# Queries of batches 2 to 7 from a transposed x, with row statistics gathered once, in an attention and mixture-of-experts kernel

## The reference

```python
x = x + _L0_xattn_ref(_layernorm(x), ctx_1024, ctx_1024, Wq, Wk, Wv, Wo)
x = x + _L0_ffn_ref(_layernorm(x), gate_w, Wg, Wu, Wd, Ws_g, Ws_u, Ws_d)

# _L0_xattn_ref, with B, L, E = 8, 512, 256, H, D = 16, 16 and 1601 context rows
q = (query @ Wq.T).reshape(B, L, H, D) * scale
k = (key @ Wk.T).reshape(B, -1, H, D)
v = (value @ Wv.T).reshape(B, -1, H, D)
scores = sigmoid(einsum('blhd,bshd->bhls', q, k))
o = einsum('bhls,bshd->blhd', scores, v).reshape(B, L, E)
return o @ Wo.T
```

## Time and profile before

| | us |
|---|---|
| median of 3 runs | 1428.64 (1427.55 to 1428.79) |
| the profiled execution's own time | 1423.46 |
| its span | 1421.7 |
| PE busy | 1360.4, 96% |
| ACT busy | 957.4, 67% |
| DVE busy | 647.7, 46% |
| first stage, attention | from 0 to about 975 |

### The profile page before, as it was taken

The page is one execution under the profiler, slowest core; times in us unless marked ns, Lnnn a source line. Parts: engine busy times, 40 slices in busy tenths (PEclk is TensorE's granted clock), DMA queues, the critical chain, the costliest instruction groups (busy, mean ns, idle before and its releaser), DMA issues.

```text
span 1421.7 us, 22246 instructions
## 1 busy us (share of the span) xinstructions
PE 1360.4 (96%) x8906; PEld 783.3 (55%) x8906; DVE 647.7 (46%) x1294; ACT 957.4 (67%) x1073; POOL 211.2 (15%) x173
## 2 busy tenths in 40 slices
PE   4879999999999999999999999998999999999995
PEld 3434444444444435344444443325888888888885
DVE  4434244234235324424523531204449677777772
ACT  3547988888888887888888889994232344444441
POOL 1000000000000000000000000020000336666654
PEclk9989999999999999999999999999999999999998
DMA  6473765586387478467548627623343465666653
GB/s 171 122 164 112 118 126 148 107 150 156 101 136 161 127 124 147 137 118 149 146 109 135 170 69 122 134 73 133 132 132 108 134 175 148 150 151 148 149 97 38
DMA packets 97160, 185.82 MB, mean 131 GB/s; under 512 B 16992, under 2 KB 51296, under 8 KB 97056
## 3 DMA queue, kind: packets, MB, share of 16 engines
q1 hardware_dynamic: 80768, 154.08, 45.5%
q0 software_dynamic: 16000, 29.91, 10.2%
q10 hardware_dynamic: 288, 0.39, 0.2%
HBM read 118.99 MB, written 61.83 MB: 127 GB/s over the span
## 4 chain that ended last, share of the span: by engine, by line
PE 86%; ACT 4%; DVE 4%; issue 2%; DMA 2%; SPq 1%; POOL 0%; POOLq 0%; DVEq 0%
PE acc L1291 24%; PE score L1331 18%; PE score L1267 17%; PE score L1346 9%; PE misc L1182 6%; PE misc L1195 5%; ACT probs L679 4%; PE misc L1218 2%; PE misc L1203 2%; PE misc L1210 1%; DMA key_scr<-key_parts 1%; PE misc L1226 1%; DVE o_sum L859 1%; SPq L388 1%; PE acc L1358 1%
## 5 line engine op out<-in xcount | busy, mean ns | idle before, releaser
L679 ACT ACTIVATE probs<-score 128x1024 f32<-128x1024 f32 (+1 forms) x832 | 789.4, 1043 | 162.8 <-PE score L1267 158.0
L1291 PE MATMUL acc<-probs,values 128*32 128x512 f32 (+1 forms) x3328 | 411.2, 600 | 4.5 <-DVE o_sum L859 3.3
L1267 PE MATMUL score<-queries,keys 48*128 48x512 f32 (+1 forms) x1664 | 315.2, 451 | 3.4 <-DMA keys<-key_parts 2.4
L1267 PEld LDWEIGHTS score<-queries,keys 48*128 48x128 f32 (+1 forms) x1664 | 128.3, 180 | 258.1 <-ACT probs L679 201.5
L688 ACT ACTIVATE gelu<-score 128x512 f32<-128x512 f32 x96 | 57.1, 594 | 209.9 <-PE score L1331 209.8
L1291 PEld LDWEIGHTS acc<-probs,values 128*32 128x32 f32 (+1 forms) x3328 | 82.9, 109 | 183.8 <-issue 143.6
L576 POOL DMA_DIRECT2D ctx_raw<-ctx_t x32 | 23.4, 731 | 754.7 <-DVE ctx_lo L767 753.8
L778 DVE CAST key_parts<-misc 128x512 fp32r<-128x512 f32 (+1 forms) x63 | 36.2, 574 | 206.9 <-PE misc L1182 195.4
L1331 PE MATMUL score<-tok_hi,gu_hi 128*128 128x512 f32 x384 | 119.8, 393 | 0.0
L1331 PE MATMUL score<-tok_lo,gu_hi 128*128 128x512 f32 x384 | 119.3, 392 | 0.0
L1331 PE MATMUL score<-tok_hi,gu_lo 128*128 128x512 f32 x384 | 118.7, 391 | 0.0
(11 more groups left out here) (158 smaller groups left out, 1382.5 us busy)
## 6 DMA issues: line engine op xcount, KB each, us to landing
keys<-key_scr SPq DMA_DIRECT2D x180, 200.2 KB, 8.0
key_scr<-key_parts SPq DMA_DIRECT2D x45, 512.0 KB, 4.4
gu_raw<-w_gu SPq DMA_DIRECT2D x17, 1024.0 KB, 6.4
ctx_raw<-ctx_t POOLq DMA_DIRECT2D x24, 512.0 KB, 4.1
queries<-query_scr SPq DMA_DIRECT2D x180, 64.0 KB, 2.7
d_raw<-w_d SPq DMA_DIRECT2D x17, 512.0 KB, 9.0
query_scr<-query_parts SPq DMA_DIRECT2D x15, 512.0 KB, 4.5
xn<-x SPq DMA_DIRECT2D x8, 512.0 KB, 3.8
```

The source lines that it names most:

```text
L679: act.activation(probs[0:rows, n % RING, 2 * pair:2 * pair + 2, :], score[k % 3][0:rows, :, :], ACT.Sigmoid, scale=SCALE).then_inc(probs_d ...
L1267: mm = pe.matmul(score[k % 3][0:rows, g, :], keys[quarter % KEY_RING][of, pair, P * st:P * st + rows], queries[half][of, e, pair, :], star ...
L1291: mm = pe.matmul(acc[32 * c:32 * (c + 1), :], values[b % 2][0:rows, st, half, c, :], probs[0:rows, n % RING, c, :], start=(st == 0), stop= ...
```

## The change

The wrapper passes x a second time, transposed per batch (`x_t`). T tasks remain for batches 0 and 1 only. In batch 1 DVE reads the rows of the six batches 2 to 7 one after another through the one buffer `xn` and keeps their means and variances (`row_sums`, at q = 0, 3, 6, 9, 12, 15); SP issues the next load of x at q = 1, 4, 7, 10, 13, each once the sums before it are done. `row_scales` at q = 15 makes all the scales; a new task M at q = 17 transposes means and scales on PE, and SP writes them to DRAM. From then on SP, at task G of batch b, loads `x_t` of the next batch and two rows of 512 numbers broadcast to all partitions, and DVE at q = 29 norms the transposed x in place and splits it for Q, which moves from q = 30 to q = 35. The tasks behind it move too.

```diff
 def beside(b):
-        at_quad = (0, 2, 8, 10, 12, 14, 16, 18, *range(26, QPB, 2))
+        at_quad = (0, 2, 8, 10, 12, 14, 16, 18, 26, 28, 30, 32, 35, 37, 39, 42, 44)
...
-                 ("T", c, 0), ("T", c, 1), ("Q", c, 0),
+                 *([("T", c, 0), ("T", c, 1), ("Q", c, 0)] if c == 1 else []),
                  ("K", c, 0, 2), ("K", c, 1, 2), ("V", c, 2, 0), ("V", c, 2, 1),
+                 *([("Q", c, 0)] if c > 1 else []),
                  ("K", c, 0, 3), ("K", c, 1, 3), ("V", c, 3, 0), ("Q", c, 1)]
+    if b == 1:
+        tasks[STATS_AT + 2] = ("M",)
...
             def load_x(b):
-                sp.wait_ge(misc_copied, COUNT["T", b - 1, KC - 1])
+                if b <= 2:
+                    sp.wait_ge(misc_copied, COUNT["T", b - 1, KC - 1])
+                else:
+                    sp.wait_ge(x_summed, b - 2)
                 sp.dma_start(xn[:], x_rows[b]).then_inc(x_in, 16)
+            def load_x_t(b):
+                if b == 2:
+                    sp.wait_ge(x_summed, B - 2)
+                else:
+                    sp.wait_ge(x_t_split, b - 2)
+                sp.dma_start(x_turned, x_t[b].rearrange("(k p) s -> p k s", p=P)).then_inc(x_t_in, 16)
+            def load_stats(b):
+                sp.wait_ge(stat_written, 16)
+                sp.wait_ge(misc_copied, COUNT["G", b - 2])
+                sp.wait_ge(nt_stored, STORE * (b - 1))
+                for which in range(2):
+                    sp.dma_start(nt_lo[:, which, :].bitcast(F32),
+                                 stat_scr[which, b].rearrange("t p -> (t p)").partition_broadcast(P)
+                                 ).then_inc(stat_in, 16)
...
@@ SP, the loop over b and q @@
                         stack_keys(4 * b + 3)
+                    if b == 1 and 0 < q <= STATS_AT and q % STATS_STEP == 1:
+                        load_x(3 + q // STATS_STEP)
...
                         elif task == ("G", b - 1):
                             load_resid_a(b)
+                            if b + 1 < B:
+                                load_x_t(b + 1)
+                                load_stats(b + 1)
                             place_gates(b - 1)
...
+            def row_sums(b):
+                dve.wait_ge(x_in, 16 * (b + 1))
+                for t in range(TT):
+                    dve.bn_stats(x_bn[:, t, :], xn[:, t, :]).then_inc(ln_step, ln.up())
+                dve.wait_ge(ln_step, ln.now())
+                for t in range(TT):
+                    last = dve.bn_aggr(stat_mv[:, TT * b + t, :], x_bn[:, t, :])
+                last.then_inc(x_summed, 1)
+            def row_scales():
...
+                dve.tensor_copy(stat[:, 0, some], stat_mv[:, some, 0]).then_inc(stat_ready, 1)
+            def normed_queries(b):
+                dve.wait_ge(x_t_in, 16 * (b - 1))
+                dve.wait_ge(stat_in, 32 * (b - 1))
+                for which, op in enumerate((ALU.subtract, ALU.mult)):
+                    dve.tensor_tensor(x_turned, x_turned,
+                                      nt_lo[:, which, :].bitcast(F32).unsqueeze(1).to_broadcast([P, KC, S]), op
+                                      ).then_inc(x_t_step, xs.up())
+                    dve.wait_ge(x_t_step, xs.now())
+                dve.tensor_copy(nt_hi[:], x_turned).then_inc(x_t_step, xs.up())
+                dve.wait_ge(x_t_step, xs.now())
+                dve.tensor_tensor(nt_lo[:], x_turned, nt_hi[:].bitcast(F32), ALU.subtract).then_inc(x_t_split, 1)
...
@@ DVE, the loop over b and q @@
-                    if b + 1 < B and q == (17 if b == 0 else 15):
-                        first_sums(b + 1)
-                    if b + 1 < B and q == (19 if b == 0 else 17):
+                    if b == 0 and q == 17:
+                        first_sums(1)
+                    if b == 0 and q == 19:
                         norm_scale()
-                    if b + 1 < B and q == (21 if b == 0 else 19):
+                    if b == 0 and q == 21:
                         norm_apply(xn, xn, xn_ready)
+                    if b == 1 and q <= STATS_AT and q % STATS_STEP == 0:
+                        row_sums(2 + q // STATS_STEP)
+                    if b == 1 and q == STATS_AT:
+                        row_scales()
+                    if 0 < b < B - 1 and q == 29:
+                        normed_queries(b + 1)
...
@@ PE, product(task) @@
+                elif kind == "M":
+                    pe.wait_ge(stat_ready, 1)
+                    mm = pe.transpose(misc[0:2 * B * TT, 0:P], stat.rearrange("p w r -> p (w r)"), ident[:])
                 elif kind == "Q":
+                    wait_past(pe, x_t_split, b - 1)
```

More of the change, by code:

```diff
@@ L74 @@
 FIRST = BEFORE[:4]
+STATS_AT, STATS_STEP = 15, 3
 def beside(b):
@@ L159, in wait_past, with build @@
         engine.wait_ge(sem, value)
-def build(nc, x, ctx_t, w_attn, gate_t, w_gu, w_d, out):
+def build(nc, x, x_t, ctx_t, w_attn, gate_t, w_gu, w_d, out):
     with ExitStack() as keep:
@@ L177, in build @@
         query_scr = [[dram(f"query_scr{p}{g}", (2, P, S), F32) for g in range(2)] for p in range(2)]
+        stat_scr = dram("stat_scr", (2, B, TT, P), F32)
         resid_scr = dram("resid_scr", (B, P, TT, D), F32)
@@ L223, in build @@
         slot_w = sb("slot_w", [P, TT, E])
+        x_bn = sb("x_bn", [P, TT, nc.vector.BN_STATS_DIM])
+        stat_mv = sum4[:, :, 0:2]
+        stat_var, stat_sq, stat_c, stat_bits = row_max, row_sum, row_inv, sum2[:, :, 0].bitcast(I32)
+        stat = top_row[:, 0, 0:2 * B * TT].rearrange("p (w r) -> p w r", w=2)
+        stat_t = sum4[0:2 * B * TT].rearrange("p r c -> p (r c)")
         gather_row = [sb(f"gather_row{p}", [P, TT], U32) for p in range(2)]
@@ L304, in build @@
         xn_ready = sem("xn_ready")
+        x_summed = sem("x_summed")
+        stat_ready = sem("stat_ready")
+        stat_written = sem("stat_written")
+        stat_in = sem("stat_in")
+        x_t_in = sem("x_t_in")
+        x_t_step = sem("x_t_step")
+        x_t_split = sem("x_t_split")
         norm_ready = sem("norm_ready")
@@ L350, in build @@
         STORE = 32
+        x_turned = xn[:].rearrange("p t d -> p (t d)").rearrange("p (k s) -> p k s", s=S)
         x_rows = x.rearrange("(b t p) d -> b p t d", b=B, p=P)
@@ L490, in _ @@
                                 stack_queries(task[1], 0)
-                        elif task[0] == "T" and task[2] == KC - 1 and task[1] + 1 < B:
+                        elif task[0] == "T" and task[2] == KC - 1:
                             load_x(task[1] + 1)
+                        elif task == ("M",):
+                            sp.wait_ge(misc_copied, COUNT[task])
+                            sp.dma_start(stat_scr.rearrange("w b t p -> (w b t) p"), stat_t
+                                         ).then_inc(stat_written, 16)
                         elif task == ("N", b - 1, 0):
@@ L748, in _ @@
             ln = Count()
+            xs = Count()
             def split_weight(w):
@@ L852, in first_sums @@
                 norm_sums(xn)
+            def row_sums(b):
[7 more added lines that the diff above has]
+            def row_scales():
+                dve.wait_ge(x_summed, B - 2)
+                some = slice(2 * TT, TT * B)
+                dve.tensor_scalar(stat_var[:, some], stat_mv[:, some, 1], EPS, None, ALU.add
+                                  ).then_inc(ln_step, ln.up())
+                dve.wait_ge(ln_step, ln.now())
+                dve.tensor_scalar(stat_bits[:, some], stat_var[:, some].bitcast(I32), 1, None,
+                                  ALU.logical_shift_right).then_inc(ln_step, ln.up())
+                dve.wait_ge(ln_step, ln.now())
+                dve.tensor_scalar(stat[:, 1, some].bitcast(I32), stat_bits[:, some], -1.0, float(0x5F3759DF),
+                                  ALU.mult, ALU.add).then_inc(ln_step, ln.up())
+                for _ in range(3):
+                    dve.wait_ge(ln_step, ln.now())
+                    dve.tensor_tensor(stat_sq[:, some], stat[:, 1, some], stat[:, 1, some], ALU.mult
+                                      ).then_inc(ln_step, ln.up())
+                    dve.wait_ge(ln_step, ln.now())
+                    dve.scalar_tensor_tensor(out=stat_c[:, some], in0=stat_sq[:, some], scalar=-0.5,
+                                             in1=stat_var[:, some], op0=ALU.mult, op1=ALU.mult
+                                             ).then_inc(ln_step, ln.up())
+                    dve.wait_ge(ln_step, ln.now())
+                    dve.scalar_tensor_tensor(out=stat[:, 1, some], in0=stat_c[:, some], scalar=1.5,
+                                             in1=stat[:, 1, some], op0=ALU.add, op1=ALU.mult
+                                             ).then_inc(ln_step, ln.up())
+                dve.memset(stat[:, :, 0:2 * TT], 0.0).then_inc(ln_step, ln.up())
+                dve.wait_ge(ln_step, ln.now())
+                dve.tensor_copy(stat[:, 0, some], stat_mv[:, some, 0]).then_inc(stat_ready, 1)
@@ L888, in copy_out @@
             def copy_out(task):
```

(8 more changed lines are left out.)

## The result

| | before, us | after, us |
|---|---|---|
| median | 1428.22 (1427.55 to 1428.79, 4 runs) | 1449.12 (1447.17 to 1451.70, 4 runs) |
| the profiled execution's own time | 1423.46 | 1451.70 |
| its span | 1421.7 | 1449.9 |
| PE, DVE busy | 1360.4, 647.7 | 1361.8, 639.8 |

The change makes the kernel 20.9 us slower: a ratio of 1.0148, 95% interval 1.0130 to 1.0165. 1451 was forecast.

The account below looks back on a forecast made before the run. PE's own instructions were taken to bound the kernel. Holds 13.5 and 9.2, half clock 4.4, middle 0.2 and M 0.2, less 4.8 won, give 22.7 us on 1428.6: 1451 us, range 1439 to 1461.

Parts of the forecast that it names:

- x of batch 3, issue to landing: Batch 1, SP's queue: the load, issued behind query and key transfers and a write, lands after 9.4 us.
- first hold: Batch 1, O product at q = 6: PE waits 13.5 us for DVE, which waits for x of batch 3.
- half clock after it: Batch 1, behind each hold: PE runs at a granted clock of 0.50, costing 2.2 us more per hold.
- middle, and M: Batch 1: DVE's sums delay the context split, 0.2 us; M on PE costs 0.2 us.
- x of batch 7, issue to landing: Batch 1, SP's queue: the load, issued behind six key transfers, lands 9.4 us later, at 219.7.
- second hold: Batch 1, before M: PE waits 9.2 us for DVE's sums, scales and V copy behind x of batch 7.
- won in each of six batches: Batches 1 to 6: two T tasks fewer win 0.8 us a batch, 4.8 us in all.
- norming of the transposed x: DVE at q = 29 of every batch: hidden, cost zero, with one us left before PE waits.
- rival (a): Batch 1: loads of x land as if alone, holds 7.9 and 3.5 us, 1440 us; chance 0.13 with its in-between.
- the second stretch of the earlier trace: Read as batch 7, few tasks left: ACT busy 120.6 us, a quad costs what ACT needs.
- lone and joined quads without a task: Batches 1 to 6: two lone quads cost 1.66 us each, two joined to the end run 3.62; gain 0.87.

Follow-up runs that it names:

- e5: Changed kernel without the loads of x for batches 3 to 7, DVE's sums, scales and M kept (wrong values): 1422.05 us, 0.9968 of the kernel before.
- e4: Changed kernel with only the load of x for batch 3 issued from POOL's queue, no earlier than before: 1448.01 us, one run.
- e3: Changed kernel with the loads of x for batches 3 and 7 both issued ahead of the stack transfers: 1434.33 us, 1.0050 of the kernel before.
- e6: e5 with the tasks on their old even quads from 30 on and the four quads without a task together at 26 to 29: 1435.10 us, one run.
- e2: Changed kernel with only the load of x for batch 7 moved ahead of the six key transfers: 1441.72 us, one run.
- e1: Changed kernel with only the load of x for batch 3 moved ahead of the query and key transfers of batch 1: 1440.38 us, one run.
- e8: Changed kernel with the six sums and their loads spread over batches 0 and 1: 1421.92 us, 0.9963 of the kernel before.
- e9: Changed kernel with the edits of e8 and the task places of e6: 1433.75 us, 1.0044 of the kernel before.

## Why the prediction was right

| step | forecast, us | profiled execution, us |
|---|---|---|
| x of batch 3, issue to landing | 9.4 | 9.9 |
| first hold | 13.5 | 13.75 |
| half clock after it | 2.2 | 2.3 (6.40 against 4.13 at full clock) |
| middle, and M | 0.4 | no wait of PE; 0.5 left over in batch 1 |
| x of batch 7, issue to landing | 9.4 | 10.1 |
| second hold | 9.2 | 9.67 |
| half clock after it | 2.2 | 3.0 (7.36 against 4.36 in e5) |
| won in each of six batches | 0.8 | 0.97 (batches 2 to 6) |
| norming of the transposed x | hidden | hidden |

Batch 1 is 144.68 - 116.49 = 28.2 us longer than before. The holds and their half clock are 28.7 of it, the gain takes 0.97 off, and 0.5 is what is left over.

- The size and the sign came from one thing: following a load of 512 KB to its place in SP's program, and taking its landing from the neighbours at that place instead of from its own median of 3.8 us. e5 shows that all the rest of what is added costs 1.3 us.
- The mechanism was right in what it did to PE, and too narrow in one word. The load is late since it is issued behind 18 transfers, but another queue doesn't help (e4), so "on the same queue" is not what decides. The rival (a), with loads that land as if alone, gave 1440 and did not come about in the kernel as written. e3 shows that moving these two loads does not bring it about either: with one ahead of the stacks, the next one is behind them.
- One reading was loose without touching the sum: the second stretch of the earlier trace rows, read as batch 7, has 50 of its 130 us in batch 6. From 870 to 950, in batch 7 alone, ACT is busy 77.5 of 80 us, so that the reading holds.
- The gain was 0.17 us a batch larger than forecast, inside its bounds. e6 does not bear out how the forecast got it, by what lone and joined quads without a task cost: by that rule four joined quads win 7.81 - 6.71 = 1.10 us and those of the change 0.87, and batch 2 shows 0.80 and 0.97. That the size was near is in part luck.
- The sum by the trace: batches 1 to 6, from the last scores of batch 0 to those of batch 6, took 722.11 us after (898.43 - 176.32) and 698.76 before (870.25 - 171.49), 23.35 more, for 22.7 forecast. The difference of the medians is 20.9. The 2.45 us between the two are less than the 5.6 us by which batch 0 differs among the profiles, but no run ties them to it. So the mechanism rests on the holds read from the trace, and the last 2 us between 1449 and 1451 say nothing about it.

## What to carry to other kernels

Where an in-order engine waits for a load and another's work stands behind it, what the load costs here is set by the transfers issued ahead of it, on its own queue or on another, and by how soon it is wanted; read its landing from neighbours in time, not from its median. Spreading the same loads, so that those behind a burst are wanted late, turned 21 us lost into 5 won, with no instruction less. When one load is moved ahead of a burst, follow the next one that depends on it too.

## What the runs showed of the hardware that was not expected

- A load issued from POOL's queue at a busy time landed after 9.4 us, like one on SP's queue (9.9). It had no packet on the engines for more than 6 us, in which SP's queue held them at 97% (e4).
- The length of one hold does not tell whether a stretch at half clock follows. Behind holds of 1.77 us (e2) and 1.84 us (e6) it came, behind one of 0.9 us before M it did not (e5). But the same hold of 2.47 us near the program's start (for `w_lo`, at 21 to 22 us) was passed at a granted clock of 1.00 in the kernel before, in e1, e3 and e4, and with a fall to 0.50 in the kernel after, in e2, e5, e6, e8 and e9.
- What a hold cost beyond itself was 2.3 us after 13.75, 3.0 after 9.67 and 2.2 after 8.79: among these three it does not grow with the hold.
